# Adding the causal mask with a matmul instead of a VectorE add, in the attention of a post-norm layer

## The reference

```
scores = jnp.einsum('bhqd,bhkd->bhqk', q_full, k_full) * scale
causal = jnp.triu(jnp.ones((s, s), dtype=bool), k=1)
scores = jnp.where(causal, -jnp.inf, scores)
attn = jax.nn.softmax(scores.astype(jnp.float32), axis=-1)
out = jnp.einsum('bhqk,bhkd->bhqd', attn, v)
```

## Time and profile before

| | us |
|---|---|
| median of 3 runs | 1889.14 (1888.12 to 1890.75) |
| the profiled execution, its own time | 1888.21 |
| its span, first to last instruction | 1886.5 |
| PE busy | 1725.7 (91%) |
| DVE busy | 1393.6 (74%) |
| ACT busy | 1096.9 (58%) |
| POOL busy | 971.9 (52%) |

### The profile page before, as it was taken

One profiled execution on the slowest core, in us unless ns is written; L12 is line 12 of the kernel. 1 busy time (PEld: TensorE's weight loads), 2 busy tenths in 40 slices (PEclk: granted clock), 3 DMA queues, 4 the chain that ended last, 5 costly groups with the idle time before them and its releaser, 6 DMA issues. The chain is left out here.

```text
span 1886.5 us, 28030 instructions
## 1 busy us (share of the span) xinstructions
PE 1725.7 (91%) x8729; PEld 1396.3 (74%) x8729; DVE 1393.6 (74%) x2503; ACT 1096.9 (58%) x2092; POOL 971.9 (52%) x883
## 2 busy tenths in 40 slices
PE   5995699999999999999988899999999999998586
PEld 4564578888888888888877688888887887886442
DVE  1552368888888888878766588888888888888366
ACT  2553256666676666657545566666666766666220
POOL 2320135555555555556543455565555665556455
PEclk9997899999999999999989899999999999999889
DMA  7876212121211311112121221212112111100321
GB/s 231 305 304 211 64 49 62 46 68 40 92 50 57 98 60 52 61 51 84 57 67 34 94 75 36 67 39 96 49 53 101 42 48 35 52 31 31 123 73 56
DMA packets 90138, 152.99 MB, mean 81 GB/s; under 512 B 17872, under 2 KB 60368, under 8 KB 87632
## 3 DMA queue, kind: packets, MB, share of 16 engines
q1 hardware_dynamic: 81168, 103.60, 17.5%
q0 software_dynamic: 7104, 23.60, 3.8%
q10 hardware_dynamic: 1728, 24.12, 3.0%
HBM read 87.30 MB, written 51.38 MB: 74 GB/s over the span
## 5 line engine op out<-in xcount | busy, mean ns | idle before, releaser
L1320 POOL TENSOR_TENSOR split_p<-pool,split_p 128x512 fp32r<-128x512 f32 x544 | 702.9, 1294 | 542.3 <-ACT split_p L1265 541.9
L1143 PE MATMUL rows<-q_c,key_c 128*128 128x512 f32 x1632 | 478.9, 402 | 27.9 <-issue 15.9
L1253 ACT COPY pool<-rows 128x512 f32<-128x512 f32 x480 | 281.8, 587 | 266.7 <-PE rows L1143 264.7
L1397 DVE TENSOR_TENSOR top<-rows,top 128x512 f32<-128x512 f32 x420 | 289.0, 688 | 146.6 <-ACT pool L1253 143.5
L1412 DVE TENSOR_TENSOR pool<-bank,pool 128x512 f32<-128x512 f32 x544 | 370.1, 680 | 27.0 <-PE bank L1161 27.0
L1258 ACT ACTIVATE pool<-pool 128x512 f32<-128x512 f32 x544 | 345.9, 636 | 18.8 <-DVE pool L1412 18.3
L1265 ACT CAST split_p<-pool 128x512 fp32r<-128x512 f32 x544 | 333.2, 612 | 25.0 <-PE bank L1174 25.0
L1143 PEld LDWEIGHTS rows<-q_c,key_c 128*128 128x128 f32 x1632 | 290.4, 190 | 76.2 <-issue 27.1
L1143 PE MATMUL rows<-q_pe,key_pe 128*128 128x512 f32 x1088 | 339.1, 393 | 0.0
L1424 DVE TENSOR_TENSOR bank<-bank,pool 128x512 f32<-128x512 f32 x480 | 331.1, 690 | 0.1
L1143 PEld LDWEIGHTS rows<-q_pe,key_pe 128*128 128x128 f32 x1088 | 205.7, 189 | 45.6
(11 more groups left out here) (159 smaller groups left out, 2058.8 us busy)
## 6 DMA issues: line engine op xcount, KB each, us to landing
cq<-cq_dram SPq DMA_DIRECT2D x28, 768.0 KB, 5.0
y<-y_dram SPq DMA_DIRECT2D x64, 256.0 KB, 3.0
y_dram<-y SPq DMA_DIRECT2D x64, 256.0 KB, 2.0
wq_dram<-wq ACTq DMA_DIRECT2D x4, 2304.0 KB, 11.5
wo_dram<-wo ACTq DMA_DIRECT2D x4, 2048.0 KB, 10.6
q_pe<-by_sin SPq DMA_DIRECT2D x256, 32.0 KB, 1.8
q_pe<-by_cos SPq DMA_DIRECT2D x256, 32.0 KB, 1.8
table<-table_dram SPq DMA_DIRECT2D x31, 256.0 KB, 2.9
```

The costliest lines, as they stand in the source:

```text
L1143: mm = pe.matmul(by_head(out), k, q, start=(z == 0), stop=(z == 4))
L1253: nc.scalar.copy(slot(n), SCORES[n % N_SCORES]).then_inc(scores_copied, 1)
L1320: nc.gpsimd.tensor_tensor(split_p[:, n % 2, 1, :], slot(n), stored(split_p[:, n % 2, 0, :]), ALU.subtract).then_inc(p_lo, 1)
L1397: nc.vector.tensor_tensor(out, SCORES[n % N_SCORES], slot(number(it, 0)) if t == 1 else out, ALU.max).then_inc(scores_maxed, 1)
```

## The change

The diagonal tile gets a sixth matmul, in bf16: stationary `mask16`, moving `ident16` read four times over (512 columns), accumulated in the same bank as the five others. ScalarE copies the diagonal tile as it copies the others, and VectorE's `masked` is gone, and with it `mask_t`, its matmul and its copy at the start. The bank of a diagonal tile is given back by ScalarE's copy (`scores_copied`) instead of `scores_maxed`; `maxed_count` replaces `copied_count`, since now every tile is copied and only the others are counted by the maximum.

```
-        mask_t = sb("mask_t", [P, P])
...
-        def copied_count(it, t):
+        def maxed_count(it, t):
 
             return FIRST[it] - it + t
...
+            def maxed(tile):
+
+                if tile[1]:
+                    pe.wait_ge(scores_maxed, maxed_count(*tile))
+                else:
+                    pe.wait_ge(scores_copied, number(*tile) + 1)
+
             def scores(it, t):
...
-                    pe.wait_ge(scores_maxed, n - N_SCORES + 1)
+                    maxed(TILES[n - N_SCORES])
...
+                if t == 0:
+                    terms.append((m.mask16[:, :], m.ident16[:, :].rearrange("p (h n) -> p h n", h=1)
+                                  .broadcast_to([P, HG, P])))
                 for z, (k, q) in enumerate(terms):
-                    mm = pe.matmul(by_head(out), k, q, start=(z == 0), stop=(z == 4))
+                    mm = pe.matmul(by_head(out), k, q, start=(z == 0), stop=(z == len(terms) - 1))
                 mm.then_inc(scores_ready, 1)
...
             def turn_max(it):
                 u = ("turn_max", it)
                 shared(u)
-                pe.wait_ge(scores_maxed, finished(it))
+                maxed(last_tile(it))
...
-            pe.matmul(MAXES[:, 0:P], m.mask16[:, :], m.ident16[:, :], start=True, stop=True).then_inc(mask_turned, 1)
-            pe.wait_ge(mask_copied, 1)
...
-                elif what == "max" and at[1] > 0:
+                elif what == "max":
                     copy_scores(*at)
...
-            def masked(it):
-                n = number(it, 0)
-                dve.wait_ge(scores_ready, n + 1)
...
-                nc.vector.tensor_tensor(by_head(slot(n)), by_head(SCORES[n % N_SCORES]),
-                                        mask_t[:, :].rearrange("p (a n) -> p a n", a=1).broadcast_to([P, HG, P]),
-                                        ALU.add).then_inc(scores_maxed, 1)
-
             def max_of(it, t):
                 n, out = number(it, t), top[:, it % 2, :]
-                dve.wait_ge(scores_copied, copied_count(it, t))
+                dve.wait_ge(scores_copied, n + 1)
                 if t == 1 and it >= 2:
 
                     dve.wait_ge(max_turned, it - 1)
-                dve.wait_ge(scores_maxed, n)
+                if t > 1:
+                    dve.wait_ge(scores_maxed, maxed_count(it, t) - 1)
...
-            dve.wait_ge(mask_turned, 1)
-            nc.vector.tensor_copy(mask_t[:, :], MAXES[:, 0:P]).then_inc(mask_copied, 1)
-            dve.wait_ge(mask_copied, 1)
```

More of the change, by code:

```diff
@@ L922, in attention_phase @@
         y_ready = sem("y_ready")
-        mask_turned = sem("mask_turned")
-        mask_copied = sem("mask_copied")
         scores_ready = sem("scores_ready")
@@ L1448, in _ @@
                     add_y(*at)
-                elif what == "max" and at[1] == 0:
-                    masked(at[0])
-                elif what == "max":
+                elif what == "max" and at[1] > 0:
                     max_of(*at)
```

## The result

The changed kernel takes 1900.55 us (median of 6, 1897.33 to 1902.43) against 1891.59 us for the kernel before in the same measurement (median of 6): ratio 1.0047, 95% interval 1.0032 to 1.0062, so +9 us, slower. A second measurement gave 1899.34 against 1891.59, ratio 1.0046 (1.0032 to 1.0060). The forecast was 1902, slower, with a sum of +13.3 us; the direction and the time held, and a third of the sum did not arrive (+13.3 lies above the interval of +6 to +12 us). That the time came so close is partly luck: the kernel before stood at 1891.59 us in this measurement, 2.5 us above the 1889.14 from which the forecast was added up. The profiled execution took 1901.91 us with a span of 1900.2.

What follows compares the result with a forecast made beforehand. The prediction took a full TensorE to bound the kernel: 14.7 for 64 matmuls, +0.7 at the lower clock, -1.4 hidden, -0.65 at the start, sum +13.3, forecast 1902 us, with 8 in 10 between 1895 and 1910.

Steps and rivals of the forecast that it cites:

- What bounds the kernel: Steady stretches: TensorE is full, so each added matmul delays all that follows, and work taken from another engine gives nothing back.
- The price of a mask matmul, 0.23 us: Diagonal tiles: each of 64 added matmuls costs the fp32r distance of starts at 512 columns, 14.7 us in all.
- (a): Rival at the diagonal tiles: bf16 between fp32r costs a change, 0.39 us per matmul, 25.0 us, so 1912; 1 in 10.
- (b): Rival at the diagonal tiles: mask matmul near the 0.12 us of 256 columns, 7.7 us, so 1895; 1 in 10.
- Hidden matmuls: Two ahead of rotary DMA waits and four ahead of y steps cost nothing, 1.4 us off.
- Elsewhere ... a wait just moves: At all other diagonal tiles the matmul precedes both PE's next work and the chain, so nothing more is hidden.
- The start, -0.65 us: Kernel start: without PE's mask matmul and the wait for VectorE's copy, the first projection starts at 176.38 instead of 177.03.
- I cost both at nothing: Move from VectorE (loses 43.5 us) to ScalarE (gains 37.6 us): claimed to leave the kernel's time unchanged.
- Rival (c): Y steps: VectorE's later steps come 0.6 us sooner and the 29.6 us of waits go, so 1872; 1 in 16.
- Rival (d): Values: ScalarE's copy makes the rounding 0.3 us late in half the iterations, +9.6 us, so 1912; 1 in 10.
- The clock as a scatter around zero: Lower-clock stretches come or go; one of 3 to 7 us moves the time by 1.5 to 3.5 us.

Runs made afterwards that it cites:

- x2: Kernel before with the bf16 mask matmul added to each diagonal tile and VectorE's mask add kept; 1903.63 us, ratio 1.0057 against the kernel before.
- x4: Changed kernel with the fifth fp32r score matmul repeated on each diagonal tile in place of the bf16 mask matmul; 1901.19 us, ratio 1.0040 against the kernel before.
- e6_after_again: Changed kernel, unchanged, measured again on the same chip as the others of its batch; 1899.34 us, ratio 1.0046 against the kernel before.
- e5_before_again: Kernel before, unchanged, measured against itself as a control; 1890.81 us, ratio 0.9993.
- e7: Changed kernel without the mask matmul, GpSimd adding the mask to the diagonal tile in the ring; 1886.94 us, ratio 0.9979 against the kernel before.
- x1: Changed kernel without its mask matmul, so the mask is left out and only the move to ScalarE remains; 1885.85 us, ratio 0.9962 against the kernel before.
- x3: Changed kernel with the mask matmul issued twice on each diagonal tile; 1915.98 us, ratio 1.0108 against the kernel before.
- e9: Kernel before, VectorE's mask add kept, with the bf16 matmul added only in iterations 26 to 35; 1891.90 us, ratio 1.0002 against the kernel before.
- e10: Kernel before, VectorE's mask add kept, with the bf16 matmul added in the 54 iterations outside 26 to 35; 1904.35 us, ratio 1.0050 against the kernel before.
- e8: Changed kernel with the mask matmul issued first of the six instead of last; 1899.39 us, ratio 1.0044 against the kernel before.

## Why the prediction came out as it did

**What bounds the kernel: right.** PE's windows are as full as before, and work added to PE shows at its full distance.

**The price of a mask matmul, 0.23 us: right.** The changed kernel's records give 0.92 us for four starts, and x2 gives 0.25 us each over 18. (a), the change of type, and (b), a price near that of 256 columns, are refuted by the same rows and by x4. The Trainium skill's sustained figure of 131 ns ("TensorE: Matmul & The Clock Gate", "Back-to-back issue gap") did not come up here either; the trace's 0.23 us stands near its isolated gap of about 216 ns.

**Hidden matmuls: right where counted, and five were missed.** The wait of 0.54 us became 0.29, and in x2 all four y steps that were named have waits shorter by a mask matmul's length. "Elsewhere ... a wait just moves" was wrong in five places of x2, 1.2 us together.

**The start, -0.65 us: not told apart.** The two profiled executions enter the attention 1 us apart (177.03 and 178.02), and the first projections run partly at the lower clock.

**"I cost both at nothing": the step that failed first.** The move is worth -7.2 us when it is alone, and 2.3 of these are waits that shortened; -0.65 was forecast for its start, and its mean clock (0.9738 against 0.9723 for the kernel before on its chip) stands for 1 to 3 more. I had argued that between the mask add and the normalising step VectorE waits for PE anyway, from one long iteration. In short iterations VectorE has no such pause, its normalising step comes 0.8 us sooner, and the values profit. Rival (c) had this mechanism, mostly at the wrong wait and more than 10 times too large: the y waits fell by 1.6 us, not by 29.6, and 0.9 of the 1.6 are the four hidden matmuls. Rival (d) did not happen; the first values matmuls waited 1.0 us in all for the rounding in e6_after_again, against 1.3 in e5_before_again.

**The clock as a scatter around zero: the step that failed second.** I counted stretches at the lower level as something that comes or goes by chance, 1.5 to 3.5 us. With one part of the change alone the mean clock is hardly above the control's 0.9734 (0.9736 to 0.9740); with the move and a matmul it is 0.9757 to 0.9770 in every run: 11 to 14 us less at the lower level for the changed kernel, worth 3 to 7. But e7, which has the move and no mask matmul among the scores, has 0.9760 as well, so the matmul is not what the higher mean needs. Beside e5_before_again the waits of PE at the full clock in e6_after_again are shorter by 4.1 us in all, where the prediction had counted 0.9 for the four y steps: 3.2 more, for the move and the other hidden matmuls together. The sum of +13.3, less 3.2 for the waits, less 3 to 7 for the clock, plus 1.9 at the weights of the next group, gives 5 to 9, against +9 measured. The terms for the waits and the weights are from single traces, the one for the clock from the means, and together they are no better than 2 us.

**Open.** The two parts alone add up to +3.6 us (-7.2 and +10.8), and the whole measures +9. The gap of 5 us is about as large as the three intervals together allow, and no term above explains it. Why the clock stays up at the group boundary with waits of the same lengths is not settled either. What differs there is when the waits come; no run moves that alone. The traces of x1, x2, x3, e7, e9 and e10 keep one or two of the three stretches; the four traces of kernels with the move and just one added matmul (the changed kernel twice, x4 and e8) have none. That place is not the whole of the mean clock: x3 and e7 have means of 0.9758 and 0.9760 and keep two of the stretches.

## What to carry to other kernels

Where one engine is full over long stretches, an operation moved onto it costs its distance of starts times its count, less those that hide in waits (x2: +10.8 us), and here the relief elsewhere did not pay for it (x1: -7.2 us); the engine with the most idle time is the better place, even at twice the duration (GpSimd's 1.29 us against 0.23 on TensorE and 0.68 on VectorE). Before the relief of another engine is set to zero, its queue should be read in the short iterations and at the boundaries, not in the steady part alone. And the granted clock of those places is part of the sum: both kernels' stretches at the lower level are to be listed, since their difference was as large as half of the effect.

## What was not expected of the hardware

A fp32r matmul behind a bf16 one is recorded as starting 0.04 us after it and lasting 0.58 us instead of 0.39, while the matmul after that stands where it would anyway (0.92 us for four). The same is seen with the bf16 matmul first or last of the bank's group, and not with an fp32r matmul in its place. And of kernels whose waits at one place are alike to 0.1 us, one loses the full clock there three times, in both of its traces, and another never, in both of its own. A transfer of the same weights at the same place took 8 us in seven of the twelve traces and 9.5 to 10.2 us in the other five, and PE waited for it each time.
